# Expert stage of a two-layer transformer kernel: transposes of the next expert issued between row tiles of the outputs, finer waits, and one weight load moved into the attention

## The reference

```python
# S = 2048 tokens, E = 8 experts, K = 2, C = 640 slots per expert, d = 256, f = 1024
dispatched = xr[dispatch_mask.reshape(-1) % S].reshape(E, C, d)
h = jax.nn.relu(jnp.einsum('ecd,edf->ecf', dispatched, w1))
expert_out = jnp.einsum('ecf,efd->ecd', h, w2)
```

## Time and profile before

| | us |
|---|---|
| runs, median (lowest to highest) | 1158.6 (1156.45 to 1159.6) |
| the profiled execution, its own time | 1155.63 |
| its span in the trace | 1153.9 |
| PE busy in the span | 968.6 (84%) |
| expert stage: first transpose to last output copy | 348.2 to 606.6 |

### The profile page before, as it was taken

The page is one execution under the profiler, slowest core; times in us unless marked ns, Lnnn a source line. Parts: engine busy times, 40 slices in busy tenths (PEclk is TensorE's granted clock), DMA queues, the critical chain, the costliest instruction groups (busy, mean ns, idle before and its releaser), DMA issues. The chain is left out here.

```text
span 1153.9 us, 17845 instructions
## 1 busy us (share of the span) xinstructions
PE 968.6 (84%) x6250; PEld 768.9 (67%) x6250; DVE 606.4 (53%) x1783; ACT 465.5 (40%) x830; POOL 460.3 (40%) x432
## 2 busy tenths in 40 slices
PE   2699999987418999999990589989999879999996
PEld 1366666754317999999990356666666557888885
DVE  5576687876613323333333477676656324553534
ACT  0155555644104333333336144645556533433322
POOL 3534644355541233223336234445243524524332
PEclk9699999988858999999995788989999989999998
DMA  3343312110125223333103462432421010000001
GB/s 132 119 157 106 113 29 94 54 41 10 42 78 187 100 90 111 118 118 118 47 12 126 158 196 92 147 115 63 148 78 56 1 46 1 1 20 1 19 1 36
DMA packets 50023, 91.78 MB, mean 80 GB/s; under 512 B 7328, under 2 KB 22944, under 8 KB 49824
## 3 DMA queue, kind: packets, MB, share of 16 engines
q1 hardware_dynamic: 46880, 82.49, 21.5%
q0 software_dynamic: 3072, 8.39, 2.3%
HBM read 54.55 MB, written 36.31 MB: 79 GB/s over the span
## 5 line engine op out<-in xcount | busy, mean ns | idle before, releaser
L775 ACT ACTIVATE a_probs<-a_ps_b 128x512 f32<-128x512 f32 x320 | 188.0, 599 | 190.5 <-PE a_ps_b L839 186.0
L823 PE MATMUL a_ps_a<-a_k_st,a_q_st 128*128 128x256 f32 (+3 forms) x512 | 204.0, 440 | 18.7 <-DMA a_k_st<-scratch 17.3
L1043 DVE CUSTOM_DVE_ANT_0 a_masked_s<-a_ps_a,a_mask_f 128x512 f32<-128x512 f32 (+1 forms) x256 | 155.6, 622 | 98.9 <-PE a_ps_a L823 93.8
L473 POOL TENSOR_SCALAR_AFFINE_SELECT a_probs<-a_probs 128x512 f32<-128x512 f32 x128 | 80.5, 643 | 200.7 <-ACT a_probs L775 200.5
L823 PEld LDWEIGHTS a_ps_a<-a_k_st,a_q_st 128*128 128x128 f32 x512 | 102.1, 202 | 80.4 <-issue 43.1
L1642 POOL TENSOR_TENSOR w_lo<-w_raw,w_hi 128x2048 fp32r<-128x2048 f32 x16 | 73.8, 4616 | 186.5 <-ACT w_hi L1660 186.5
L839 PE MATMUL a_ps_b<-a_q_less,a_k_st 128*128 128x384 f32 (+3 forms) x512 | 139.0, 335 | 4.5 <-ACT a_probs L775 3.7
L839 PEld LDWEIGHTS a_ps_b<-a_q_less,a_k_st 128*128 128x128 f32 x512 | 91.0, 196 | 28.3 <-ACT a_probs L775 19.1
L1668 ACT ACTIVATE exp_h_hi<-exp_ps_u 128x320 fp32r<-128x320 f32 x128 | 49.1, 437 | 148.4 <-PE exp_ps_u L1732 148.4
L863 PE MATMUL a_ps_pv<-a_probs,a_v 128*32 128x512 f32 (+3 forms) x1024 | 93.7, 465 | 12.3 <-POOL a_probs L473 12.3
L1697 DVE SCALAR_TENSOR_TENSOR exp_h_lo<-exp_ps_u,exp_h_hi 128x320 fp32r<-128x320 f32 x128 | 56.9, 486 | 69.4 <-ACT exp_h_hi L1668 69.4
(11 more groups left out here) (259 smaller groups left out, 2298.9 us busy)
## 6 DMA issues: line engine op xcount, KB each, us to landing
w_raw<-in_m_w SPq DMA_DIRECT2D x16, 1024.0 KB, 5.1
scratch<-a_hi SPq DMA_DIRECT2D x24, 512.0 KB, 2.8
scratch<-a_lo SPq DMA_DIRECT2D x24, 256.0 KB, 3.1
a_q_st<-scratch SPq DMA_DIRECT2D x64, 96.0 KB, 2.6
a_k_st<-scratch SPq DMA_DIRECT2D x64, 96.0 KB, 2.6
exp_rows<-dispatched SPq DMA_DIRECT2D x9, 640.0 KB, 4.0
results<-exp_out SPq DMA_DIRECT2D x8, 640.0 KB, 2.9
dispatched<-kept_sub SPq DMA_DIRECT2D x9, 512.0 KB, 2.9
```

What stands on the lines that cost most here:

```text
L473: nc.gpsimd.affine_select(out=blocks, in_=blocks, compare_op=ALU.is_ge, fill=0.0, base=0, pattern=[[0, HPG], [1, P]], channel_multiplier=- ...
L775: nc.scalar.activation(probs[:, k, :], ps_b[k % B_BANKS][:, :], ACT.Exp, scale=scale).then_inc(exps, 1)
L823: last = nc.tensor.matmul(ps[:, at:at + wd], q_st[t % STACKS][:, h // PER_TILE, i * P:wd], k_st[t % STACKS][:, h, 0:wd], start=True, stop= ...
L1043: nc.vector.tensor_tensor_reduce(masked_s[n % 2][:, 0:wd], ps[:, 0:wd], mask_f[:, SEQ - wd:SEQ], -1.0, -NEG, ALU.add, ALU.min, nmax[:, t % ...
```

## The change

It has five parts.

- In `hidden` the two halves of a block are no longer interleaved: 6 matmuls of one half, then 6 of the other, each half with its own wait for its bank.
- `transposes` and `outputs` are called piece by piece. After row tile 0 come the wait for the next rows and fill 0, after tile 1 fill 1, after tile 2 fill 2. ScalarE does `t_upper` of fill 0, then rounds w1, then does fills 1 and 2. VectorE does `t_lower` of fill 0, output copy 0, `t_lower` of 1 and 2, copies 1 and 2.
- Row tile 0 waits block by block for the first half of h; the wait for all of h stands before tile 1.
- w2 of expert 0 is loaded by SP in the first attention at T = 12, and SP waits for it at that stage's end. The raw tile of w2 is therefore allocated there. The expert stage counts it as loaded at once.
- At the start of the expert stage SP loads rows of expert 0 and waits until they have landed; then it issues rows and w1 of expert 1.

```diff
@@ attention_phase, SP
                     sp.dma_start(w1["raw"][:, :, :], w["w1"][0].rearrange("(c p) f -> p c f", p=P)).then_inc(first_in, 16)
+                if rope and T == 12:
+                    sp.dma_start(w2["raw"][:, :, :], w["w2"][0].rearrange("(c p) d -> p c d", p=P)).then_inc(second_in, 16)
...
+            if rope:
+                sp.wait_ge(second_in, 16)
@@ expert_phase, SP
+            sp.sem_inc(w2_in, 16)
             load_rows(sp, 0, 0)
-            load_weights(sp, "w2", w2, w2_in, 0)
+            sp.wait_ge(rows_in[0], 16)
             load_rows(sp, 1, 1)
@@ ScalarE, in the loop
-                    t_upper(it, p + 1)
-
+                    t_upper(it, p + 1, 0)
                     upper(w1, w1_in, it * 32 + 16 * (p + 1), w1_hi_ready)
+                    for n in range(1, T_FILLS):
+                        t_upper(it, p + 1, n)
@@ VectorE, in the loop
+                    t_lower(it, p + 1, 0)
+                    out_copy(it, p, 0)
+                    for n in range(1, T_FILLS):
+                        t_lower(it, p + 1, n)
+                    for n in range(1, O_FILLS):
+                        out_copy(it, p, n)
@@ TensorE
                     for half in range(2):
                         pe.wait_ge(u_free, fills(it, p, U_FILLS, 2 * f + half + 1))
-                    for c in range(KC):
-                        for n, (i, j) in enumerate(PASSES):
-                            for half in range(2):
+                        for c in range(KC):
+                            for n, (i, j) in enumerate(PASSES):
                                 last = nc.tensor.matmul(ps_u[(2 * f + half) % U_BANKS][:, 0:HALF],
...
+            def outputs(it, p, t):
+                if t % 2 == 0:
+                    pe.wait_ge(o_free, fills(it, p, O_FILLS, t // 2 + 1))
+                bank = ps_o[(p * O_FILLS + t // 2) % O_BANKS]
+                if t == 1:
+                    pe.wait_ge(u_free, fills(it, p, U_FILLS, U_FILLS + U_BANKS))
+                for f in range(FC):
+                    if t == 0:
+
+                        pe.wait_ge(u_free, fills(it, p, U_FILLS, U_BANKS + 2 * f + 1))
...
                     hidden(it, p)
-                    pe.wait_ge(rows_in[1 - p], it * 16 + 16 * (1 + p))
-                    transposes(it, p + 1)
-
-                    pe.wait_ge(u_free, fills(it, p, U_FILLS, U_FILLS + U_BANKS))
+
                     pe.wait_ge(w2_ready, it * PAIR + (p + 1))
-                    outputs(it, p)
+                    for t in range(CT):
+                        outputs(it, p, t)
+                        if t == 0:
+                            pe.wait_ge(rows_in[1 - p], it * 16 + 16 * (1 + p))
+                        if t < T_FILLS:
+                            transposes(it, p + 1, t)
```

More of the change, by code:

```diff
@@ L1651, in _, with t_upper @@
         def _(act):
[L1652 to L1656, removed]
+            def t_upper(it, p, n):
+                src, dst = t_block(n)
+                act.wait_ge(t_full, fills(it, p, T_FILLS, n + 1))
+                nc.scalar.copy(x_t[0][:, dst], ps_t[(p * T_FILLS + n) % T_BANKS][:, src]).then_inc(t_hi, 1)
             def upper(of, loaded, count, ready):
@@ L1681, in _, with t_lower, out_copy @@
             dve.sem_inc(o_free, O_BANKS)
[L1683 to L1690, removed]
+            def t_lower(it, p, n):
+                src, dst = t_block(n)
+                dve.wait_ge(t_hi, fills(it, p, T_FILLS, n + 1))
+                nc.vector.tensor_tensor(x_t[1][:, dst], ps_t[(p * T_FILLS + n) % T_BANKS][:, src],
+                                        x_t[0][:, dst].bitcast(F32), ALU.subtract).then_inc(t_free, 1)
+            def out_copy(it, p, n):
+                width = min(SEQ, CT * D - n * SEQ)
+                dve.wait_ge(o_full, fills(it, p, O_FILLS, n + 1))
+                if n == 0:
+                    dve.wait_ge(stored[p], it * 16 + 16)
+                nc.vector.tensor_copy(out[p][:, n * SEQ:n * SEQ + width],
+                                      ps_o[(p * O_FILLS + n) % O_BANKS][:, 0:width]).then_inc(o_free, 1)
+            for n in range(T_FILLS):
+                t_lower(0, 0, n)
             with dve.Fori(0, E0 // PAIR) as it:
@@ L1699, in _, with transposes @@
                                                        ALU.subtract).then_inc(u_free, 1)
[L1700 to L1708, removed]
+                    t_lower(it, p + 1, 0)
[4 more added lines that the diff above has]
+                        out_copy(it, p, n)
         @block.tensor
         def _(pe):
[L1712 to L1718, removed]
+            def transposes(it, p, fill):
+                pe.wait_ge(t_free, fills(it, p, T_FILLS, fill + 1))
+                bank = ps_t[(p * T_FILLS + fill) % T_BANKS]
+                for n in range(4 * fill, min(4 * fill + 4, KC * CT)):
                     c, t = divmod(n, CT)
@@ L1736, in hidden @@
                                                         stop=(c == KC - 1 and n == len(PASSES) - 1))
[L1737 to L1751, removed]
+                        last.then_inc(u_full, 1)
+            def outputs(it, p, t):
[7 more added lines that the diff above has]
+                        pe.wait_ge(u_free, fills(it, p, U_FILLS, U_BANKS + 2 * f + 1))
+                    for n, (i, j) in enumerate(PASSES):
+                        last = nc.tensor.matmul(bank[:, t % 2 * D:(t % 2 + 1) * D], h[i][:, f, t * P:(t + 1) * P],
+                                                (w2["hi"], w2["lo"])[j][:, f, :], start=(f == 0 and n == 0),
+                                                stop=(f == FC - 1 and n == len(PASSES) - 1))
+                if t % 2 or t == CT - 1:
+                    last.then_inc(o_full, 1)
             pe.wait_ge(rows_in[0], 16)
-            transposes(0, 0)
+            for fill in range(T_FILLS):
+                transposes(0, 0, fill)
             with pe.Fori(0, E0 // PAIR) as it:
@@ L2153, in program @@
                 norm_phase(nc, keep)
-                attention_phase(nc, keep, first, 0, route, w1, early)
-            w2 = {part: moe.enter_context(nc.sbuf_tensor(f"w2_{part}", [P, FC, D], F32 if part == "raw" else F32R))
-                  for part in ("raw", "hi", "lo")}
+                attention_phase(nc, keep, first, 0, route, w1, w2, early)
+            w2 |= {part: moe.enter_context(nc.sbuf_tensor(f"w2_{part}", [P, FC, D], F32R)) for part in ("hi", "lo")}
             expert_phase(nc, keep, experts, w1, w2)
```

13 lines of the change are left out of this document (7 added, 6 removed).

## The result

The changed kernel took 1138.64 us in the median of 4 runs (1137.67 to 1145.59), the kernel before 1158.67 (1156.45 to 1159.6): ratio 0.9843, 95% interval 0.9801 to 0.9885. Two later comparisons of the same two kernels, on other chips, gave 0.9903 (0.9867 to 0.9938) and 0.9892 (0.9865 to 0.9919), with medians 10.9 and 9.5 us apart. The mean of the three ratios is 0.988, 14 us. So there are two questions: what the change is worth, and what moves one comparison against another by 10 us.

What follows compares the result with a forecast made beforehand. PE's queue was taken to bound the expert stage. Changeover 1.0 plus stall 0.5 gives 1.5 us per expert, 12.0 for eight: 1158.6 - 12.0 = 1146.6 us, range 1142 to 1152.

Steps and rivals of the forecast that it cites:

- the two waits: PE's waits once per expert: transposes for DVE's x_t lo, 1.0 us, and a hidden block for h lo, 0.5 us.
- Halves in sequence: In hidden, PE's stall behind ACT's rounding goes wholly: 0.50 us per expert, with 0.2 us to spare.
- Finer waits: Before the outputs, the block-by-block waits for h are covered by other matmuls and cost nothing of their own.
- w2's lo part: POOL's operation, the next limit before the outputs: 1.7 us of cover, beyond which each us late is lost per expert.
- the bank wait: At the changeover PE waits for a free ps_t bank before the third fill; spreading transposes behind row tiles removes it.
- The changeover after: Hidden to outputs: ten transposes plus three returns cost 1.4 us in place of 2.4, so 1.0 us less per expert.
- The 0.09: Price in us of one return from transposes to fp32r matmuls, taken from the attention's rows.
- The end of 1.15: Low end of the changeover's cost after the change, 1.15 us, from the attention's groups priced with their returns.
- The dear end: Rival at the changeover: each return costs 0.17 us, changeover 1.6 us, time 1148.2; smaller gains together had chance 0.22.
- Moved load, stage start, order on ACT, DVE, SP and POOL: w2's first load in the attention, the wait for expert 0's rows, reordered work of other engines: 0 us each.
- Larger gains: Outcome with more time saved than the forecast's 1144 to 1148 us: chance 0.02.

Runs made afterwards that it cites:

- e2: Changed kernel with the halves in hidden interleaved again: period 30.05 us, ratio to the kernel before 0.9919.
- e1: Kernel before with only the halves put in sequence: period 30.81 us, ratio 0.9978.
- e6: Changed kernel with w2 rounded behind the tenth half in place of the sixth: ratio to the kernel before 1.01, periods 31.6 and 33.3 us in turn.
- e4: Changed kernel with the coarse wait for every half of h before row tile 0: period 30.89 us, ratio to the kernel before 0.9983.
- e5: Changed kernel with its ten transposes in five groups of two in place of 4, 4, 2: 1140.94 us, ratio to the kernel before 0.9875.
- e3: Kernel before with only SP's part, w2's first load moved into the first attention and the wait for expert 0's rows: period 31.38 us, ratio 0.9999.
- e8: e7 with 50 unread matmuls at the expert stage's start and 14 and 16 around the third fill: 1150.41 us, ratio to the kernel before 0.987.
- e7: Changed kernel plus unread bf16 matmuls, 36 at the expert stage's start and 75 at the second attention's: 1139.4 us, ratio to the kernel before 0.9857.

## Why the prediction was right or wrong

- *PE's queue is the bound of the stage, and the two waits are what can be won.* Right: both gone, PE busy throughout, no other engine or queue came up.
- *Halves in sequence, 0.50 us.* Right (e2), 0.57 alone (e1).
- *Finer waits cost nothing and are covered; w2's lo part is next, 1.7 us away.* Right: 1.55 us (e6). But the text put the whole gain of the changeover down to the bank wait. e4 shows that the finer waits are needed for it: with the coarse one the new wait takes 1.34 us, all of the 1.33 that the spread and the finer waits bring together (e2).
- *The changeover after, "1.1 + 3 x 0.09 = 1.4 us".* Wrong, and this is the step of the sum that failed. It measured 1.10, so the changeover gave 1.3 us in place of 1.0 and the period 1.83 in place of 1.5, which is 2.6 us over eight experts. The 0.09 was read rightly and added wrongly. In the same rows four transposes take 0.36, not 4 x 0.11 = 0.44; the 0.11 is the distance between two transposes inside a group, and the last one of a group has a shorter one. Price the group with its return, 0.45, and there is nothing to add. The end of 1.15 in the prediction did just that and was passed over for the middle. e5 shows the same with five groups.
- *The dear end of 0.165 to 0.17 at a return*: refuted by e5. The Trainium skill, "TensorE: Matmul & The Clock Gate", Part 4 (PE-mode transpose), has about 275 ns for a transpose in a kernel's context; the rows after show 0.27 us from start to end too, and none of it is paid as a tail.
- *Moved load, stage start, order on ACT, DVE, SP and POOL: 0 each.* Right (e3, and the rows after).
- *The time and the range.* The stages that the change touches give 14.6 + 0.2 = 14.8 us, so 1158.6 would become 1143.8, inside the range. The measured 20.0 holds 5.2 us more, of which 3.1 stand in the profiles: 3.0 in the second attention, where the clock came back sooner, 0.6 in the first, -0.5 in the dense stage. The clock accounts for most of that: the two traces differ by 181.9 - 174.8 = 7.1 us at 1.2 GHz, an estimate of 2.6 us by the 0.36 of the runs. The rest, 2.1 us, lies in the difference between medians of four and single profiled executions; 1.8 of the 20.0 go when the means are taken, and the later comparisons don't show such a surplus. The failed step is 2.6 of the 8.0 us by which the forecast was short; with it put right the measurement would lie 5.2 us below the middle. The other part is an error of the range: it took the spread for 3 us, from three runs 3 us apart, and the same kernel before ran from 1150.3 to 1170.6 over the later comparisons. Larger gains had a chance of 0.02, which was too small for that reason alone. Where the forecast of 12.0 comes near the later 10.9 and 9.5, that is luck: the stage gave 14.6, and more time at 1.2 GHz took some 3 us back.

## What to carry to other kernels

Time a stage by its period, from start to start in the profile: it is exact to 0.01 us here, where totals of the same two programs gave gains of 9.5, 10.9 and 20.0 us. When totals must serve, note each run's mean granted clock and compare at equal time at the low level: here that took the gain from 10.8 and 11.4 us to 13.9 and 14.3. Price a group of instructions from the start of its first to the start of the second one behind it, and never add a part of that row to a figure that stems from inside the group. When work moves out of a gap, ask what the gap hid: here it was the wait for h, and the move paid only with the finer waits.

## What the runs showed of the hardware that was not expected

- Ten 128x128 fp32 transposes among fp32r matmuls cost 0.11 us each with the switching, in groups of 4, 4 and 2 or in five groups of 2 (period 29.55 us in both, e5).
- A wait of PE costs the idle time that the profile names and about 0.26 us besides: 0.50 for a bracket of 0.24 in hidden, 1.3 for 1.04 between transposes, 1.34 for 1.09 before outputs (e4), 2.06 for 1.80 (e6).
- In a stage that is otherwise busy a wait of 1.98 us brought the clock down to 1.2 GHz for some 3.4 us, 1.5 us more (e6, in three of six periods); the wait of 1.99 in expert 0 did not, nor did those of 1.80 in the periods between, nor the waits of 1.04 in the kernel before.
- One program spends 58 to 82 us of the second attention at 1.2 GHz, from one execution to another and without a cause that these runs show. Each us goes with 0.395 us of that stage, and over whole runs of the kernel before with 0.35 to 0.42 us of total.
- Matmuls that nothing reads brought the first products to 2.4 GHz where they also filled the waits of about 1 us in between (e8, first period 29.64 us in place of 32.34); with those left open the clock fell back (e7, 31.71).
